# The first attention of a transformer layer: the transposed row maxima in a score bank, VectorE copying the second head's row, and the norm between the stages in pieces

## The reference

```
x = x + ln(attention(ln(x)))          # 16 heads of 16, causal, then Wo
x = x + ln(block(ln(x)))              # block: rmsnorm, 16-head causal attention with heads of 128,
                                      # rmsnorm, a gate that picks 4 of 16 experts, shared and routed MLPs
```

```
sim = (q @ k.T) * 16 ** -0.5;  sim = where(causal, sim, -inf)
weights = softmax(sim);        out = (weights @ v) @ Wo.T
```

## Time and profile before

| | |
|---|---|
| median of 3 runs (lowest, highest) | 1367.52 us (1364.16 to 1369.35) |
| the profiled execution: its time, its span | 1366.35 us, 1364.6 us |
| busy in the span | PE 87%, DVE 64%, ACT 59%, POOL 41% |
| first attention, 61 to 335 us: TensorE busy | 210 of 274 us, at a granted clock of 0.78 to 0.90 of full |
| second attention, 440 to 500 us: TensorE busy | 58.9 of 60 us, at a granted clock of 1.00 |

### The profile page before, as it was taken

How to read it: one execution, slowest core, us unless ns; L and a number is a source line. 1 busy time by engine, 2 the same in 40 slices (tenths; PEclk the granted TensorE clock), 3 DMA queues, 4 the chain that set the end, 5 groups by cost and what they waited for, 6 DMA issues and landing times.

```text
span 1364.6 us, 24173 instructions
## 1 busy us (share of the span) xinstructions
PE 1192.3 (87%) x7548; PEld 1001.8 (73%) x7548; DVE 868.4 (64%) x2550; ACT 807.7 (59%) x1992; POOL 559.9 (41%) x901
## 2 busy tenths in 40 slices
PE   4888777776899999999999999999997869999930
PEld 3744333344799899899999999999986749999930
DVE  7465545452567676678777787777865845555546
ACT  2466555554666777767867678776676524444412
POOL 3052524242542443543754236543362333444434
PEclk9999888787999999999999999999999989999975
DMA  3477555540015101111220113201022233333353
GB/s 134 122 225 235 179 160 156 166 132 31 24 61 152 63 32 62 43 52 62 80 78 32 62 35 107 78 32 62 32 85 84 76 100 110 118 118 118 117 218 121
DMA packets 93296, 134.93 MB, mean 99 GB/s; under 512 B 11093, under 2 KB 71765, under 8 KB 93045
## 3 DMA queue, kind: packets, MB, share of 16 engines
q1 hardware_dynamic: 86308, 114.51, 26.6%
q0 software_dynamic: 6864, 18.88, 3.8%
HBM read 65.45 MB, written 55.18 MB: 88 GB/s over the span
## 4 chain that ended last, share of the span: by engine, by line
PE 68%; DVE 9%; ACT 9%; POOL 5%; issue 4%; DMA 2%; SPq 2%; another core or an unknown queue 0%; POOLq 0%; ACTq 0%; DVEq 0%
PE bank L1413 46%; PE bank L1800 5%; PE bank L1492 4%; PE bank L1618 4%; PE bank L1463 2%; ACT pT L797 2%; DVE bank L1073 2%; PE bank L1486 2%; ACT stk L802 1%; PE bank L1779 1%; PE bank L1479 1%; PE bank L1810 1%; ACT p L909 1%; DVE hs L1268 1%; DMA yl<-ys_rows 1%
## 5 line engine op out<-in xcount | busy, mean ns | idle before, releaser
L1073 DVE CUSTOM_DVE_ANT_0 bank<-bank,mask 128x512 f32<-128x512 f32 (+3 forms) x512 | 236.1, 523 | 76.4 <-PE bank L1479 57.5
L900 ACT ACTIVATE p<-bank,stat 128x512 f32<-128x512 f32 (+3 forms) x256 | 131.5, 526 | 131.1 <-DVE stat L1073 131.1
L1413 PE MATMUL bank<-xT,w_hl 128*128 128x512 f32 x768 | 190.2, 396 | 2.0 <-DVE hs L1268 1.7
L488 POOL CAST w_hl<-raw_qkv 128x512 fp32r<-128x512 f32 x96 | 58.6, 610 | 315.0 <-DMA raw_qkv<-in_qkvo 166.1
L1413 PEld LDWEIGHTS bank<-xT,w_hl 128*128 128x128 f32 x768 | 144.1, 188 | 37.5 <-issue 2.1
L797 ACT ACTIVATE pT<-bank 128x512 f32<-128x512 f32 x160 | 87.9, 599 | 96.4 <-PE bank L1486 95.9
L1413 PE MATMUL bank<-pT,v 128*128 128x128 f32 (+3 forms) x768 | 137.5, 328 | 0.0
L1413 PE MATMUL bank<-qk 128*128 128x512 f32 (+3 forms) x768 | 130.8, 319 | 5.3 <-DVE pT L1255 5.3
L909 ACT ACTIVATE p<-p,stat 128x512 f32<-128x512 f32 (+3 forms) x256 | 123.1, 552 | 15.2 <-DVE stat L1271 15.0
L1413 PEld LDWEIGHTS bank<-qk 128*128 128x128 f32 x768 | 120.4, 190 | 14.3 <-DVE v L1249 3.8
L700 POOL DMA_INDIRECT ys_rows<-mid,goal x79 | 76.4, 968 | 128.2 <-DVE mid L1370 125.6
(11 more groups left out here) (239 smaller groups left out, 2500.9 us busy)
## 6 DMA issues: line engine op xcount, KB each, us to landing
xs_rows<-blank SPq DMA_DIRECT2D x31, 1040.0 KB, 4.8
raw_qkv<-in_qkvo SPq DMA_DIRECT2D x32, 768.0 KB
xrow<-xs_rows SPq DMA_DIRECT2D x79, 130.0 KB, 2.1
raw_o<-in_qkvo SPq DMA_DIRECT2D x32, 256.0 KB
yl<-ys_rows SPq DMA_DIRECT2D x16, 512.0 KB, 9.5
stk<-xT SPq DMA_DIRECT2D x96, 64.0 KB
stk<-k_hl SPq DMA_DIRECT2D x96, 64.0 KB
w_raw<-in_moe SPq DMA_DIRECT2D x12, 320.0 KB, 5.1
```

Of the source, the lines that this page charges most:

```text
L488: pool.tensor_copy(hi, raw).then_inc(b_half, 1)
L900: act.activation(p2[:, n % 2, POFF[qi]:POFF[qi + 1]], s2(t), ACT.Exp, scale=-1.0, bias=stat2[:, 0, n % 2, t:t + 1], accum_out=stat2[:, 1, ...
L1073: return dve.tensor_tensor_reduce(scores, scores, mask[:, TB - scores.shape[1]:], scale=-1.0, scalar=-2.0 * MASKED, op0=ALU.add, op1=ALU.m ...
L1413: ins = pe.matmul(out, a, b, start=start and i == 0, stop=stop and i == len(pairs) - 1, **kw)
```

## The change

- TensorE transposes the maxima into bank `st1(s, 0)` (one of the three for the scores by key) and not into the free bank. For that it waits for the third exponential of step s - 1, and no longer for the users of the free bank. These waits are moved to the other users of the free bank.
- ScalarE copies the row of head 0, VectorE that of head 1 (after the maxima of the first score part of s + 1).
- TensorE's wait for the two row copies stands ahead of the first score product by key, behind the rest of the scores by query, the transposes of `o_sum` and the product with Wo.
- ScalarE takes the third exponential after `o_sum`, `take_y` and `scale_u`, not ahead of them.
- GpSimd's norm comes in four parts, one behind each of the four selects: the first norm at position 3 (was 2), the second at 6 (was 5). `make_x1` comes in four parts of 128x512 at position 5 (was 4). A weight split at steps 0 to 3 comes ahead of the fourth select.
- `scale_u` and `scale_xn`: two tiles on ScalarE, two on VectorE, which does them between the first and the other maxima of positions 4 and 7. `scale_hs` goes to GpSimd for the first three batches.
- Three small loads share one semaphore.

The diff, cut:

```diff
@@ GpSimd
+            def norm(b, half, part, done):
+                n = half + 1
+                if part == 0:
+                    row_moments(b, half)
+                if part == 1:
+                    first_roots(n)
+                    better_roots(n)
+                if part == 2:
+                    better_roots(n)
+                if part == 3:
+                    better_roots(n)
+                    offsets(n, done)
+            def make_x1(b, part):
+                rows = slice(2 * (part % 2), 2 * (part % 2) + 2)
+                x1, mid_ = x_sb[:, TPB * b:TPB * (b + 1), :][:, rows, :], mid[:, rows, :]
+                if part < 2:
+                    pool.wait_ge(m_ua, 2 * (b + 1))
+                    pool.wait_ge(m_ud, 2 * (b + 1))
+                    pool.tensor_tensor(mid_, x1, mid_, ALU.add).then_inc(m_x1, 1)
+                else:
+                    pool.wait_ge(m_x1, 2 * (b + 1))
+                    link(pool.tensor_copy(x1, mid_))
             def step1(s):
                 fill_v(s)
-                clear_future(s)
-                if b >= 0 and k == 2:
-                    norm_y(b)
-                if b >= 0 and k == 4:
-                    make_x1(b)
-                if b >= 0 and k == 5:
-                    norm_x1(b)
+                for i in range(4):
+                    clear_future(s, i)
+                    if s < 4 and i == 2:
+                        split_qk(0) if s == 0 else split_v() if s == 1 else split_qk(1) if s == 2 else split_o()
+                    if b >= 0 and k == 3:
+                        norm(b, 0, i, m_nrm)
+                    if b >= 0 and k == 5:
+                        make_x1(b, i)
+                    if b >= 0 and k == 6:
+                        norm(b, 1, i, m_rms)
+                    if b >= 1 and k in (0, 1) and i in (1, 3):
+                        scale_hs(b - 1, 2 * k + i // 2)
@@ ScalarE
-                    for a in range(2):
-                        act.activation(stk[64 * a:64 * a + 1, s % NSTK, 0, :], free[64 * a:64 * a + 1, :], ACT.Copy)\
-                           .then_inc(a1_m, 1)
+                    act.activation(stk[0:1, s % NSTK, 0, :], st1(s, 0)[0:1, :], ACT.Copy).then_inc(a1_m, 1)
-                    for i in range(3):
-                        exp(i)
+                    exp(0)
+                    exp(1)
...
-                    for i in range(3, 5):
+                    for i in range(2, 5):
                         exp(i)
-                if b >= 1 and k in (0, 1):
-                    scale_hs(b - 1, k)
@@ VectorE
             def x1_stats(b):
-                dve.wait_ge(m_x1, b + 1)
+                dve.wait_ge(m_x1, 2 * (b + 1))
...
+                def take_row():
+                    dve.wait_ge(a1_mt, s + 1)
+                    dve.tensor_copy(stk[64:65, s % NSTK, 0, :], st1(s, 0)[64:65, :]).then_inc(a1_m, 1)
...
                         row_max(a, n)
+                        if i == 0 and s >= 0:
+                            take_row()
...
+                if b >= 0 and s < N1 and k == 4:
+                    scale_u(b)
+                if b >= 0 and s < N1 and k == 7:
+                    scale_xn(b)
@@ TensorE
                     if s >= 1:
-                        pe.wait_ge(a1_m, 2 * s)
-                    if s >= 4 and s % 2 == 0:
-                        pe.wait_ge(a1_xo, s // 2 - 1)
-                    if s >= 6 and s % 4 == 2:
-                        pe.wait_ge(a1_o, (s - 6) // 4 + 1)
...
+                        pe.wait_ge(a1_exp, 5 * (s - 1) + 3)
                     pe.wait_ge(a1_max, 6 * (s + 1))
-                    turn(lambda j: least[:, s % 2, j, :], a1_mt, free)
+                    turn(lambda j: least[:, s % 2, j, :], a1_mt, st1(s, 0))
...
-                if 0 <= s < N1:
-                    pe.wait_ge(a1_m, 2 * (s + 1))
                 if s >= 3 and s % 2 == 1:
...
                 if 0 <= s < N1:
+                    pe.wait_ge(a1_m, 2 * (s + 1))
                     for i, (a, n) in enumerate(S1_PARTS):
```

More of the change, by code:

```diff
@@ L546, in make_x1, with better_roots @@
-            def make_x1(b):
-                pool.wait_ge(m_ua, TPB * (b + 1))
-                x1, mid_ = batch_tiles(x_sb, b, 0, TPB), mid[:, :, :].rearrange("p j d -> p (j d)")
-                pool.tensor_tensor(mid_, x1, mid_, ALU.add).then_inc(m_x1, 1)
-                pool.wait_ge(m_x1, b + 1)
-                link(pool.tensor_copy(x1, mid_))
-            def norm_x1(b):
-                row_moments(b, 1)
-                roots(2, m_rms)
+            def better_roots(n):
+                r, v, t = (midst[:, i:i + n, :] for i in (RSTD, VAR, TMP))
+                link(pool.tensor_tensor(t, r, r, ALU.mult))
+                link(pool.tensor_tensor(t, t, v, ALU.mult))
+                link(pool.tensor_scalar(t, t, 1.5, None, ALU.add))
+                link(pool.tensor_tensor(r, r, t, ALU.mult))
@@ new lines, in offsets @@
+            def offsets(n, done):
+                r, o = (midst[:, i:i + n, :] for i in (RSTD, OFF))
+                pool.tensor_tensor(o, r, mean.unsqueeze(1).to_broadcast([P, n, TPB]), ALU.mult).then_inc(done, 1)
+            def norm(b, half, part, done):
[10 more added lines that the diff above has]
+                    offsets(n, done)
@@ L559, in step1, with scale_hs @@
+            def scale_hs(b, j):
+                pool.wait_ge(m_rms, b + 1)
+                pool.tensor_scalar(batch_tiles(hs, b, j), mid[:, j, :], midst[:, RSTD, j:j + 1], midst[:, OFF, j:j + 1],
+                                   ALU.mult, ALU.add).then_inc(m_hs, 1)
             def step1(s):
+                b, k = s // (N1 // B) - 1, s % (N1 // B)
                 fill_v(s)
-                clear_future(s)
-                b, k = s // (N1 // B) - 1, s % (N1 // B)
-                if s == 0:
-                    split_qk(0)
@@ L578, in _ @@
             for s in range(N1):
                 step1(s)
+            for j in range(TPB):
+                scale_hs(B - 2, j)
             meet(pool, 1)
-            norm_y(B - 1)
+            for part in range(4):
+                norm(B - 1, 0, part, m_nrm)
             steps = [0]
@@ L656, in step2 @@
                 if n == 0:
-                    make_x1(B - 1)
+                    for part in range(4):
+                        make_x1(B - 1, part)
                 if n >= H2 and n % H2 == POST_SQ:
@@ L675, in step2 @@
                 if n == 4:
-                    roots(2, m_rms)
+                    first_roots(2)
+                    better_roots(2)
+                    better_roots(2)
+                    better_roots(2)
+                    offsets(2, m_rms)
                 if n == 14:
@@ L767, in scale_u @@
                 act.wait_ge(m_nrm, b + 1)
-                for j in range(TPB):
+                for j in (0, 1):
                     act.activation(mid[:, j, :], mid[:, j, :], ACT.Identity, bias=midst[:, OFF, j:j + 1],
@@ L1082, in y_stats, with scale_u, scale_xn @@
                 mid_stats(half)
+            def scale_u(b):
+                dve.wait_ge(m_nrm, b + 1)
+                for j in (2, 3):
+                    dve.tensor_scalar(mid[:, j, :], mid[:, j, :], midst[:, RSTD, j:j + 1], midst[:, OFF, j:j + 1],
+                                      ALU.mult, ALU.add).then_inc(m_ud, 1)
+            def scale_xn(b):
+                dve.wait_ge(m_rms, b + 1)
+                for j in (2, 3):
+                    dve.tensor_scalar(xn_mid[:, j, :], mid[:, j, :], midst[:, RSTD2, j:j + 1], midst[:, OFF2, j:j + 1],
+                                      ALU.mult, ALU.add).then_inc(m_xnd, 1)
             def x1_stats(b):
-                dve.wait_ge(m_x1, b + 1)
+                dve.wait_ge(m_x1, 2 * (b + 1))
                 mid_stats(0)
@@ L1294, in step2 @@
                        .then_inc(b_ol, 1)
+                if n == LAST_U:
+                    scale_u(B - 1)
                 if n == LAST_STAT:
                     x1_stats(B - 1)
+                if n == LAST_XN:
+                    scale_xn(B - 1)
                 if here and post >= 0 and n % H2 == POST_XN:
```

71 lines of the change are left out of this document (29 added, 42 removed).

## The result

The changed kernel took 1344.47 us at the median of 4 runs (1344.4 to 1346.02), the kernel before 1365.84 beside it (4 runs, 1360.52 to 1369.35): ratio 0.985 with a 95% interval of 0.981 to 0.989. The profiled execution has a span of 1342.4 us, 22.2 less than before. Of the kernel before, one execution beside e1 to e4 took 1482.81 us at a mean granted clock of 0.78 and is left out of their ratios.

What follows compares the result with a forecast made beforehand. It took the first attention as a loop of waits, plain steps through ScalarE, the norm the larger lever. The terms sum to 21.1 us off 1366.35, giving 1345.3, and 1346.5 as the runs' median; range 1339 to 1354.

Steps and rivals of the forecast that it cites:

- term A: First eight steps, without the norm: 2.2 us gained, less 0.6 for GpSimd's weight split, so 1.6 gained.
- term B: Round 2, eight steps with the norm of the batch before: 65.05 us instead of 72.0, 7.0 gained.
- C: Round 3: first six positions 44.85 us instead of 57.51, position 6 loses 4.5; 8.2 gained.
- D: Round 1, no transposes at positions 0 and 1: 63.7 us instead of 64.96, 1.3 gained.
- E: After the last round: two `scale_hs` tiles go to GpSimd, last position and step 32 shorten; 2.0 us gained.
- F: Head of the second attention: two of four ScalarE tiles ahead of TensorE's wait go; 1.0 us gained.
- (a): Rival: norm waits at positions 4, 6 and 7 each take 1.5 us longer than worked out; 1360 us, chance 0.17.
- (b): Rival: VectorE's queue is the new, slower bound in all 32 steps, deciding from 0.66 us each; 1375 us, chance 0.07.
- (c): Rival: position 6 does not stall because GpSimd reaches the additions sooner; 1334 us, chance 0.09.
- (d): Rival: VectorE and GpSimd hold each other up, 1.0 us at each of six places; 1352.5 us, chance 0.12.
- The clock: Charges for half clock behind the waits: 0.5 us at position 5, 0.3 at position 0, 1.4 at position 6.

Runs made afterwards that it cites:

- e1: Changed kernel with norm, addition and scalings put back as before, keeping only the rows part (bank, row copies, waits, third exponential): 1336.16 us, ratio 0.9766 to before.
- e4: Changed kernel with VectorE's row copy made twice, first into a spare row: 1359.03 us, ratio 0.9951 to the kernel before.
- e9: The changed kernel as it is, run again on the third group's chip: 1346.26 us, ratio 0.984 to the kernel before.
- e6: Changed kernel with VectorE's two scalings at positions 4 and 7 behind the other maxima: 1326.32 us, ratio 0.9792 to the kernel before.
- e3: Changed kernel with both rows copied by ScalarE from the score bank, none by VectorE: 1334.51 us, ratio 0.9769 to the kernel before.
- e5: Changed kernel with `x1_stats` moved from the end of position 5 to between the maxima of position 6: 1320.46 us, ratio 0.975 to the kernel before.
- e8: Changed kernel with the third exponential again ahead of `o_sum`, `take_y` and `scale_u`: 1341.68 us, ratio 0.9913 to the kernel before.
- e7: Changed kernel with VectorE's row copy behind the second score part's maxima instead of the first's: 1332.59 us, ratio 0.9841 to the kernel before.
- e11: Changed kernel with the edits of e5 and e3 together: 1328.3 us, ratio 0.9715 to the kernel before.

## Why the prediction was right

The time was forecast as 1346.5 and measured as 1344.5; the gain between the profiles was forecast as 21.1 us and measured as 22.2. That the sum came out within 1.1 us is in part luck: term A fell 1.4 short and round 3 0.6, while the tail of the first attention came out 1.4 better than worked out, the head of the second 1.2 and round 1 0.4.

- *Plain steps, term A (1.6): mis-sized, 0.2 by the start of step 8, 0.5 if counted from the start of step 0.* The mechanism holds, the loop moved to VectorE. Each piece came late by a little: transposes at +0.73 instead of +0.65, the copy 0.69 instead of 0.65, the end 2.32 after the scores by key instead of 2.26. Steps 4 to 7 took 23.99 instead of 23.6. The other half I got by doubling, while steps 0 to 3, partly at half clock in both kernels, took 25.02 us instead of 24.75; step 0 itself starts 0.25 later in this profile, but not in e9.
- *A round with the norm, term B (7.0): 7.15.* Round 2 was worked out as 13.25, 9.0, 5.9, 9.8, 6.9, 20.2 and measured 13.75, 8.92, 6.12, 9.47, 7.20, 19.39. The product with Wo starts at +2.47 of position 2 (+2.5). Position 4 is as long as worked out for a reason that the sum did not have: its products at half clock, not VectorE's maxima, end last there (e6). Waits in front of VectorE at position 4 end at +7.46 (worked out +7.6); at position 6 the second addition ends at +2.57 (+2.6) and the scores by key start at +6.68 (+6.65).
- *Round 3 and 1, terms C and D (8.2, 1.3):* the six positions gained 12.1 (12.7 worked out), round 1 1.7. *E and F:* from step 30 to the last product with Wo 1.1 was lost (4.5 - 2.0 = 2.5 worked out). The two timelines divide it: 5.3 lost up to the transposes of step 31, 0.4 in step 31, and 4.5 gained from the first value product of step 32 on (8.8 instead of 13.3 us), where 2.0 was worked out. Behind that product 2.2 was gained (1.0); why, no run tested.
- *Rivals.* (a) did not come; the waits were about as long as worked out, and position 7 was a microsecond shorter (VectorE's wait ends at +7.13 there, not +7.6). (b) is right in its mechanism, by e4 and e3: VectorE's queue bounds the plain steps, at +0.37 in even ones, under the 0.66 from which it decides. (c) is refuted by the 3.05 us wait; e5 shows what its absence is worth, 12 to 13 us where I had worked out 12. (d) did not happen on the path, see the last section.
- *What the prediction did not see* is how the gain divides. It named the norm as the larger lever and credited positions 0, 1, 2 to transposes that no longer wait, 5 to ScalarE's lighter load. By e1 the rows part alone is worth 31 us, and the norm part takes about 10 back, though position 5 is shorter by it. Part of what the rows part gave at positions 1 and 3 came from the later third exponential (e8), whose new place the prediction charged as a cost in the odd steps. I had the prices of positions 4 and 6 right and still read them as part of a gain, since I compared with before and not with the other half of the change.
- *The clock.* I charged 0.5 at position 5 and 0.3 at position 0 as fixed. The runs show nearly full clock or 1.3 to 1.8 us more: e9 against the first profile of the same kernel. What decides it is open; in their profiles most of what e6, e7 and e11 missed of their sums lies there.

## What to carry to other kernels

When work is cut up and strewn into an in-order queue, look at what stands behind each piece that waits: the statistics at position 6 and `y_stats` in e8 each put a wait of 3 us in front of the loop's maxima, and moving the first one group later took its wait away. Where two engines end at nearly the same time, as at position 4, taking one wait away shows nothing until the other end is earlier too. Time the halves of a change apart, for a sum that comes out right can hide a part that costs. Give a copy to the engine that has slack in the loop, here ScalarE once its wait was moved, not to the one with the shorter queue before the change.

## What the runs showed of the hardware

VectorE's copy of one row and its scaling of a 128x256 tile, each a line of the changed kernel (shortest, median, longest in ns):

```profile
L1153 DVE CAST stk<-bank x32: 689/689/690, 66.7 to 298.7; 1x512 fp32r<-1x512 f32 x32
```

```profile
L1107 DVE TENSOR_SCALAR mid<-mid,midst x8: 384/454/1390, 147.7 to 330.1; 128x256 f32<-128x256 f32 x8
```

One row of 512 costs VectorE 689 ns, as much as its maxima over 128 rows, and ScalarE 570. The tile of 1390 is the one at 330.1, at the head of the second attention (L490 is a GpSimd operation of two tensors, 128x512):

```profile
329.84 1.69 DVE L1107 TENSOR_SCALAR mid<-mid,midst 128x256 f32<-128x256 f32 x2
...
329.97 1.40 POOL L490 TENSOR_TENSOR w_hl<-raw_qkv,w_hl 128x512 fp32r<-128x512 f32 x1
```

Two tiles ended at 331.53, GpSimd's instruction at 331.37: the second tile seems to have waited for the whole of it. The Trainium skill, page "SBUF — State Buffer", section Terms, has the two engines hold their common port pair for a full instruction; this pair of rows agrees. So does the one long tile of the earlier trace rows, which ran from 1054.17 beside a GpSimd operation on 128x512 of 1.28 us at 1054.09. At positions 4 and 7 nothing of this size came: two tiles took 0.82 us beside GpSimd's short instructions (0.73 at 450.3, with none beside them), and its select took 0.53 instead of the usual 0.41.
